# A new order of work on ScalarE, VectorE and GpSimd ahead of the tile loop, and the last expert call in two halves

## The chip, the cores and the metric

The kernel runs on one core of one Trainium2 chip. The metric is the device time of one execution in microseconds (us). Three runs of the kernel before gave a median of 718.08 us.

## The reference

The input is x with 8 x 256 rows of 512 numbers. Three sublayers follow each other; each adds to x what it computes from the layer norm of x. The first and the third are a mixture of 64 rank-16 experts, the second is a gated feed-forward layer in which the smaller half of each row's gate values is set to zero.

```
def ffn(x, A, B, Wr):                     # 64 experts of rank 16, the best 16 of each row
    scores = x @ Wr.T
    top_vals, top_idx = top_k(scores, 16)
    G = scatter(softmax(top_vals), top_idx)
    h = einsum('nd,krd->nkr', x, A)
    return einsum('nkr,kdr->nd', h * G[:, :, None], B) * 2.0

def attn(x, w_gate, w_up, w_down):        # I = 1376
    s = silu(x @ w_gate.T)
    s = where(|s| is among the 688 smallest of its row, 0, s)
    s = s * (x @ w_up.T)
    return s @ w_down.T

x = x + 0.5 * ffn(layernorm(x), A, B, Wr)
x = x + attn(layernorm(x), w_gate, w_up, w_down)
x = x + 0.5 * ffn(layernorm(x), A, B, Wr)
```

## The kernel before

**Tiles and precision.** The 2048 rows are 16 tiles of 128 rows (`NT = 16`). Every tile t passes sublayer 1, 2 and 3, in the code `j = 1, 2, 3`. Each operand of a matmul is held as two float16 numbers, an upper half (`hi`, made on ScalarE by `split_hi`, `x_to_hi`, `p_to_hi`, `v_to_hi`) and a lower half, the difference (`lo`, made on VectorE by `split_lo`, `x_to_lo`, `p_to_lo`, `v_to_lo`). A product takes three matmuls: hi by hi, lo by hi, hi by lo. Weights are scaled by their norm first: `square` and `norms` make the sums of squares, `read_norm` reads them, GpSimd's `make_scale` and `make_inverse` make the factors.

**The steps of a tile.** In sublayer 1 or 3: `norm_stats`, `rstd` (GpSimd), `norm_apply`, the two halves, `turn_x` (a transposing DMA that SyncE issues), `experts` (scores, then two blocks of 512 columns of the product with A), `choose`, `exps` and `route` for the weights of the experts, `apply_route` for the product `routed`, its halves, `turn_p` and `combine` (the product with B), then `add_ffn`. In sublayer 2: `gates` (1376 columns, three blocks), `tanh`, `silu` (VectorE; the result is what the code calls `gate_ready`), `ups` (three blocks), `gated` (the product `val`; `gated_begun` and `gated_ended` do its first two blocks and the third apart), `magnitude`, the search, `select`, `mask`, `check`, `v_to_hi`, `v_to_lo`, `turn_v`, `down` and `add_down`.

**The search** finds for every row the threshold below which values are zeroed. GpSimd's `aim` sets a first guess. Then seven counts on ScalarE (`count(t, n)`, a sign with a sum) alternate with six steps on GpSimd (`search(t, n)`, four operations on 128 x 1 numbers, lines 517 to 521). Each step adds 1 to `thr_ready[t % 2]`, to which `aim` adds 1 too, so that `thr_ready[0]` is 2 after `search(0, 0)`. VectorE's `select` then takes the threshold from the last count, `mask` zeroes, and TensorE sums a flag (`sum_flags`) that `check` reads.

**Who sets the order.** It is written out by hand. Each engine's block lists its steps one after the other, and each engine does its list in that order; semaphores couple the lists. A step whose operands are late holds up all that stands behind it on its engine. SyncE's list issues the DMAs in the same way. Ahead of the loop (`for d in range(1, FULL)`, ten passes of `tile(d)`) the weights are loaded and split while the first five tiles pass sublayer 1 and tiles 0 to 2 sublayer 2; the last five tiles, a, b, c, e and f, have an order of their own. The down weights (`MD`) have six pieces; the last has 96 rows. `calls` numbers the 32 calls of sublayers 1 and 3 in order, the last one is `(3, f)`.

**PSUM.** Eight banks of 512 numbers: `DOWN` 0, `COMB` 1, `WIDE` 2 to 4, `EXP` 5 and 6, `SCORE` 7.

## Time and profile before

| | us |
|---|---|
| median of 3 runs (717.94 to 718.62) | 718.08 |
| the profiled execution | 717.54 |
| its span on the core | 715.8 |
| TensorE busy, matmuls | 691.9 (97%) |
| VectorE busy | 471.3 (66%) |
| ScalarE busy | 359.8 (50%) |
| GpSimd busy | 220.2 (31%) |

A timeline row is one operation, or several alike (xcount), with its start and its length in us from the start of the span. In brackets stands how long its engine had been idle before it and what ended that. TensorE's matmuls overlap, so their lengths add up to more than the time they take. The name after the engine is the line of the kernel; `mem` is a large buffer that holds the staged weights at first and `gate`, `val`, `masked`, their halves and some x later.

### The profile page before, as it was taken

To read this page: it belongs to the slowest core of one execution; us is meant where nothing else is said; L and a number is where in the kernel's file an instruction comes from. 1 tells how busy PE (TensorE), PEld (TensorE's weight loads), DVE (VectorE), ACT (ScalarE), POOL (GpSimd) and SP (SyncE) were. 2 spreads that over 40 slices of the span, in tenths; PEclk is the share of its full clock that TensorE was granted. 3 is DMA by queue.
4 is the path that set the end of the run, shared out by engine and by line. 5 is a ranking of instruction groups with operands and counts; after the bars stand their busy time and mean duration, and the time that the engine had idled before them with its cause. 6 is when DMAs were issued, how large, how long until landed. Compare 5 with 4: busy or idle time off the path is not lost.

```text
span 715.8 us, 10349 instructions
## 1 busy us (share of the span) xinstructions
PE 691.9 (97%) x3674; PEld 331.2 (46%) x3675; DVE 471.3 (66%) x982; ACT 359.8 (50%) x466; POOL 220.2 (31%) x545
## 2 busy tenths in 40 slices
PE   4999898999999999999999999999999999999997
PEld 3444344435444454444445444444544444444443
DVE  6999756768476666756666576566747575538862
ACT  5887775644535254452535535254462536576220
POOL 3122443532414233240423315142341423344000
PEclk9999999999999999999999999999999999999999
DMA  9969304253525163351514325242442324123442
GB/s 333 307 154 214 52 11 71 44 100 81 95 49 95 30 110 64 71 102 33 102 42 100 74 57 89 47 97 44 91 69 49 67 44 86 30 55 71 86 85 78
DMA packets 171723, 62.28 MB, mean 87 GB/s; under 512 B 163632, under 2 KB 163632, under 8 KB 171664
## 3 DMA queue, kind: packets, MB, share of 16 engines
q1 hardware_dynamic: 171664, 61.56, 40.4%
q8 instruction: 29, 0.48, 0.3%
q14 instruction: 30, 0.25, 0.1%
HBM read 16.97 MB, written 4.19 MB: 30 GB/s over the span
## 4 chain that ended last, share of the span: by engine, by line
PE 64%; ACT 9%; DVE 9%; POOL 7%; issue 5%; DMA 4%; SPq 1%; DVEq 0%; POOLq 0%; ACTq 0%
PE ps L601 12%; PE ps L602 12%; PE ps L603 12%; PE ps L716 9%; PE ps L720 9%; PE ps L717 9%; ACT signs L924 5%; POOL small L521 3%; POOL small L518 1%; DMA mem<-w_d 1%; POOL small L517 1%; DMA mem<-w_a 1%; DVE routed L1216 1%; POOL small L519 1%; ACT mem L936 1%
## 5 line engine op out<-in xcount | busy, mean ns | idle before, releaser
L924 ACT ACTIVATE signs<-mem,small 128x1376 bf16<-128x1376 f32 x112 | 161.4, 1441 | 156.1 <-POOL small L521 140.5
L716 PE MATMUL ps<-w_b_hi,pt_hi 128*128 128x512 f16 x256 | 97.0, 379 | 0.6 <-DMA pt_hi<-p_hi 0.6
L717 PE MATMUL ps<-w_b_lo,pt_hi 128*128 128x512 f16 x256 | 97.0, 379 | 0.0
L601 PE MATMUL ps<-w_a_hi,xt_f 128*128 128x512 f16 x248 | 94.0, 379 | 0.0
L602 PE MATMUL ps<-w_a_hi,xt_f 128*128 128x512 f16 x248 | 94.0, 379 | 0.0
L603 PE MATMUL ps<-w_a_lo,xt_f 128*128 128x512 f16 x248 | 94.0, 379 | 0.0
L601 PE MATMUL ps<-w_u_hi,xt 128*128 128x512 f16 (+1 forms) x192 | 69.1, 360 | 4.4 <-DVE mem L1246 4.4
L517 POOL TENSOR_SCALAR small<-small 128x1 f32<-128x1 f32 x96 | 30.8, 321 | 129.6 <-ACT signs L924 128.6
L716 PE MATMUL ps<-w_d_hi,mem 128*128 128x512 f16 x176 | 66.7, 379 | 3.0 <-DMA mem<-mem 1.8
L601 PE MATMUL ps<-w_g_hi,xt 128*128 128x512 f16 (+1 forms) x192 | 68.5, 357 | 0.9 <-DVE mem L1253 0.9
L602 PE MATMUL ps<-w_u_hi,xt 128*128 128x512 f16 (+1 forms) x192 | 69.3, 361 | 0.0
L603 PE MATMUL ps<-w_u_lo,xt 128*128 128x512 f16 (+1 forms) x192 | 69.2, 360 | 0.0
L477 POOL TENSOR_SCALAR rvar<-mv 128x1 f32<-128x1 f32 x48 | 11.7, 244 | 185.8 <-DVE mv L1161 184.3
L602 PE MATMUL ps<-w_g_hi,xt 128*128 128x512 f16 (+1 forms) x192 | 68.5, 357 | 0.0
L603 PE MATMUL ps<-w_g_lo,xt 128*128 128x512 f16 (+1 forms) x192 | 68.5, 357 | 0.0
L717 PE MATMUL ps<-w_d_lo,mem 128*128 128x512 f16 x176 | 66.7, 379 | 0.0
L720 PE MATMUL ps<-w_b_hi,pt_lo 128*128 128x512 f16 x256 | 60.5, 379 | 0.0
L907 ACT ACTIVATE mem<-mem 128x512 f16<-128x512 f32 x16 | 10.0, 627 | 99.9 <-DVE mem L1168 99.9
L521 POOL TENSOR_SCALAR small<-small,steps 128x1 f32<-128x1 f32 x96 | 54.9, 572 | 10.8 <-POOL small L519 0.2
L1282 DVE SCALAR_TENSOR_TENSOR mem<-mem,small 128x1376 f32<-128x1376 f32 x16 | 26.4, 1650 | 48.3 <-ACT signs L924 48.2
L1176 DVE TENSOR_TENSOR halves<-normed,halves 128x512 f16<-128x512 f32 x30 | 20.7, 690 | 55.8 <-ACT halves L907 55.6
L1226 DVE TENSOR_TENSOR p_lo<-routed,p_hi 128x1024 f16<-128x1024 f32 x32 | 39.0, 1219 | 17.9 <-ACT p_hi L918 17.8
(142 smaller groups left out, 1210.3 us busy)
## 6 DMA issues: line engine op xcount, KB each, us to landing
x<-x SPq DMA_DIRECT2D x14, 256.0 KB, 3.5
out<-x SPq DMA_DIRECT2D x14, 256.0 KB, 2.3
mem<-w_g SPq DMA_DIRECT2D x4, 688.0 KB, 12.5
mem<-w_u SPq DMA_DIRECT2D x4, 688.0 KB, 5.6
mem<-w_d SPq DMA_DIRECT2D x5, 512.0 KB, 6.2
mem<-w_a SPq DMA_DIRECT2D x4, 512.0 KB, 6.2
mem<-w_b SPq DMA_DIRECT2D x4, 512.0 KB, 9.3
pt_hi<-p_hi SPq DMA_TRANSPOSE x32, 3.2
```

The lines of the kernel that those rows point to most:

```text
L517: link(pool.tensor_scalar(off[h], bal[h], -7.0, None, ALU.add))
L521: pool.tensor_scalar(thr[h], move[h], steps[h][:, n:n + 1], thr[h], ALU.mult, ALU.add).then_inc(thr_ready[h], 1)
L601: pe.matmul(dst, x_hi, w_hi, start=start, stop=False)
L602: pe.matmul(dst, x_lo, w_hi, start=False, stop=False)
L603: return pe.matmul(dst, x_hi, w_lo, start=False, stop=stop)
L716: pe.matmul(dst, x_hi[:, c, :], hi[m.name][:, c, :], start=c == 0, stop=False)
L717: pe.matmul(dst, x_hi[:, c, :], lo[m.name][:, c, :], start=False, stop=False)
L720: mm = pe.matmul(dst, x_lo[:, c, :], hi[m.name][:, c, :], start=False, stop=c == chunks - 1)
L924: act.activation(signs[:, :], mags[h], ACT.Sign, bias=thr[h], scale=-1.0, accum_out=bal[h]).then_inc(counted[h], 1)
L1176: dve.tensor_tensor(halves[j][:, D:2 * D], normed[j], halves[j][:, 0:D], ALU.subtract).then_inc(x_lo_ready[j], 1)
L1226: dve.tensor_tensor(p_lo[:, :], routed[:, :], p_hi[:, :], ALU.subtract).then_inc(p_lo_ready, 1)
L1282: link(dve.scalar_tensor_tensor(out=masked[:, 0:I], in0=mag, scalar=thr[h], in1=mag, op0=ALU.is_le, op1=ALU.mult))
```

## The change

1. **ScalarE.** `tanh(0)` and `p_to_hi(4)` stand behind three of the six squares of the down weights, not all six. The first search starts ahead of `x_to_hi(2, 2)`, the upper halves of the down weights (`split_hi(MD, n)`) are spread over both first searches, and `count`, `x_to_hi`, `v_to_hi` and `exps` are in another order up to tile 2. In the end phase `tanh(e)` stands ahead of `count(c, 6)`.
2. **VectorE.** Six waits on `thr_ready` are added: ahead of `p_to_lo(4)`, of four groups of steps that begin with a lower half of the down weights, and of `mask(0)`. `p_to_lo(4)`, `x_to_lo(2, 2)` and `gated(0)` are behind the first of them. `choose` and `route` of call 5 go ahead of `silu(1)` and behind `select(0)`. `select(1)` goes ahead of `norm_apply(3, 0)`, and `mask(1)` ahead of `x_to_lo(3, 0)`.
3. **GpSimd and SyncE.** `make_inverse("gud")` stands behind three search steps, `rstd(1, LEAD)` behind two, `rstd(2, 3)` behind the second search. `turn_x(2, 3)` is issued behind `turn_v(1)`.
4. **TensorE.** `norms(MD)`, six matmuls of one column, stands behind the first block of `ups(0)`.
5. **The last call** in two halves: `apply_route`, `p_to_hi`, `combine`, `add_ffn` and `store` of call `(3, f)` each in two pieces of half the width. `combine_last` has 48 matmuls of 256 columns for 24 of 512. The two transposing DMAs stay whole.

```diff
 scored, expert_done, combined = sem("scored"), sem("expert_done"), sem("combined")
+expert_begun, routed_begun = sem("expert_begun"), sem("routed_begun")
+comb_begun, added_begun = sem("comb_begun"), sem("added_begun")
+stored_begun = sem("stored_begun")
...
         sp.dma_start(out[t * P:(t + 1) * P, :], slot(t)).then_inc(stored[t % SLOTS], 16)
+    def store_last():
+        t, w = NT - 1, D // 2
+        sp.wait_ge(added_begun, 1)
+        sp.dma_start(out[t * P:(t + 1) * P, 0:w], slot(t)[:, 0:w]).then_inc(stored_begun, 16)
+        sp.wait_ge(added, len(calls))
+        sp.dma_start(out[t * P:(t + 1) * P, w:D], slot(t)[:, w:D]
+                     ).then_inc(stored[t % SLOTS], 16)
     def turn_x(j, t):
...
     turn_p(number[1, LEAD])
-    turn_x(2, 3)
...
     turn_v(1)
+    turn_x(2, 3)
...
     store(e)
-    store(f)
+    store_last()
+    sp.wait_ge(stored_begun, 16)
...
     make_scale(MD)
+    search(0, 0)
+    search(0, 1)
+    rstd(1, LEAD)
+    search(0, 2)
     make_inverse("gud", 2.0 ** -25)
-    search(0, 0)
-    rstd(1, LEAD)
-    searches(0, 1, 2, 3, 4, 5)
+    searches(0, 3, 4, 5)
     aim(1)
-    searches(1, 0, 1, 2, 3, 4)
+    searches(1, 0, 1, 2, 3, 4, 5)
     rstd(2, 3)
-    search(1, 5)
...
                                x_hi[c], x_lo[c], c == 0, c == DC - 1)
+                if o == 0 and k == len(calls) - 1:
+                    mm.then_inc(expert_begun, 1)
...
             pe.wait_ge(val_ready, NT)
-        elif k == len(calls) - 1:
-            pe.wait_ge(added, k - 1)
...
                    16 * (k + 1), fresh).then_inc(combined, 1)
+    def combine_last():
+        k = len(calls) - 1
+        pe.wait_ge(pt_hi_loaded, 16 * (k + 1))
+        pe.wait_ge(added, k - 1)
+        pe.wait_ge(x2_ready, NT)
+        x_hi, x_lo, w = pt_hi[k % 2], pt_lo[k % 2], D // 2
+        halves_of = [(bank(b, w), slice(h * w, (h + 1) * w)) for h, b in ((0, COMB), (1, DOWN))]
+        for dst, cols in halves_of:
+            for c in range(RC):
+                pe.matmul(dst, x_hi[:, c, :], hi["b"][:, c, cols], start=c == 0, stop=False)
+                pe.matmul(dst, x_hi[:, c, :], lo["b"][:, c, cols], start=False, stop=False)
+        pe.wait_ge(pt_lo_loaded, 16 * (k + 1))
+        for (dst, cols), done in zip(halves_of, (comb_begun, combined)):
+            for c in range(RC):
+                mm = pe.matmul(dst, x_lo[:, c, :], hi["b"][:, c, cols], start=False,
+                               stop=c == RC - 1)
+            mm.then_inc(done, 1)
     def wide(m, t, fresh=False, flags_of=None, norms_of=None, begun=None, behind=None):
...
         return mm
-    def gates(t, fresh=False, norms_of=None):
+    def gates(t, fresh=False):
...
             pe.wait_ge(val_ready, t)
-        wide(MG, t, fresh, norms_of=norms_of, behind=t if early else None
+        wide(MG, t, fresh, behind=t if early else None
              ).then_inc(gate_done, 1)
-    def ups(t, fresh=False, flags_of=None):
+    def ups(t, fresh=False, flags_of=None, norms_of=None):
         pe.wait_ge(gate_ready, t + 1)
-        wide(MU, t, fresh, flags_of, begun=up_begun if t in (1, NT - 2) else None
+        wide(MU, t, fresh, flags_of, norms_of, up_begun if t in (1, NT - 2) else None
...
     combine(1, 3)
-    norms(MD)
-    ups(0, fresh=True)
+    ups(0, fresh=True, norms_of=MD)
...
     combine(3, e)
-    combine(3, f)
+    combine_last()
...
         act.activation(p_hi[:, :], routed[:, :], ACT.Copy).then_inc(p_hi_ready, 1)
+    def p_to_hi_last():
+        k = len(calls) - 1
+        act.wait_ge(routed_begun, 1)
+        act.wait_ge(pt_hi_loaded, 16 * k)
+        act.activation(p_hi[:, 0:BANK], routed[:, 0:BANK], ACT.Copy)
+        act.wait_ge(routed_ready, k + 1)
+        act.activation(p_hi[:, BANK:KR], routed[:, BANK:KR], ACT.Copy
+                       ).then_inc(p_hi_ready, 1)
     def count(t, n):
...
     exps(4)
-    for n in range(len(MD.pieces)):
+    for n in range(3):
...
     p_to_hi(4)
+    square(MD, 3)
+    square(MD, 4)
     magnitude(0)
-    x_to_hi(2, 2)
+    square(MD, 5)
...
     count(0, 0)
+    x_to_hi(2, 2)
+    count(0, 1)
     split_hi(MD, 0)
-    count(0, 1)
+    count(0, 2)
...
     x_to_hi(1, LEAD)
-    count(0, 2)
+    count(0, 3)
     split_hi(MD, 2)
-    count(0, 3)
-    split_hi(MD, 3)
     count(0, 4)
-    split_hi(MD, 4)
...
     tanh(1)
-    split_hi(MD, 5)
+    split_hi(MD, 3)
+    exps(number[1, LEAD])
...
     magnitude(1)
-    counts(1, 0, 1, 2)
+    split_hi(MD, 4)
+    count(1, 0)
+    split_hi(MD, 5)
+    counts(1, 1, 2)
     v_to_hi(0)
-    exps(number[1, LEAD])
...
     p_to_hi(number[1, LEAD])
+    count(1, 4)
     tanh(2)
-    count(1, 4)
+    count(1, 5)
     magnitude(2)
-    count(1, 5)
+    count(1, 6)
+    act.wait_ge(counted[1], ROUNDS)
+    count(2, 0)
+    x_to_hi(3, 0)
+    count(2, 1)
     x_to_hi(2, 3)
-    count(1, 6)
-    x_to_hi(3, 0)
-    act.wait_ge(counted[1], ROUNDS)
-    counts(2, 0, 1, 2)
     v_to_hi(1)
+    count(2, 2)
+    exps(number[3, 0])
     count(2, 3)
-    exps(number[3, 0])
...
     p_to_hi(number[3, a])
-    counts(c, 5, 6)
+    count(c, 5)
     tanh(e)
+    count(c, 6)
...
     exps(number[3, f])
-    p_to_hi(number[3, f])
+    p_to_hi_last()
...
             ALU.mult).then_inc(routed_ready, 1)
+    def apply_route_last():
+        k = len(calls) - 1
+        halves_of = [slice(h * BANK, (h + 1) * BANK) for h in range(2)]
+        heads = [slice(h * KE // 2, (h + 1) * KE // 2) for h in range(2)]
+        for h, (of, at, done) in enumerate(((expert_begun, 1, routed_begun),
+                                            (expert_done, k + 1, routed_ready))):
+            dve.wait_ge(of, at)
+            dve.tensor_tensor(
+                routed[:, halves_of[h]].rearrange("p (k r) -> p k r", r=RANK),
+                bank(banks_of(k) + h).rearrange("p (k r) -> p k r", r=RANK),
+                weight[:, heads[h]].unsqueeze(2).to_broadcast([P, KE // 2, RANK]),
+                ALU.mult).then_inc(done, 1)
     def p_to_lo(k):
...
                                  ).then_inc(added, 1)
+    def add_last():
+        k, w = len(calls) - 1, D // 2
+        for h, (of, at, b, done) in enumerate(((comb_begun, 1, COMB, added_begun),
+                                               (combined, k + 1, DOWN, added))):
+            x = slot(NT - 1)[:, h * w:(h + 1) * w]
+            dve.wait_ge(of, at)
+            dve.scalar_tensor_tensor(out=x, in0=bank(b, w), scalar=unscale_f, in1=x,
+                                     op0=ALU.mult, op1=ALU.add).then_inc(done, 1)
     def add_down(t):
...
     read_norm(MD)
+    add_ffn(1, 3)
+    norm_stats(1, LEAD)
+    dve.wait_ge(thr_ready[0], 2)
     p_to_lo(4)
-    add_ffn(1, 3)
     x_to_lo(2, 2)
-    norm_stats(1, LEAD)
+    gated(0)
+    norm_apply(1, LEAD)
+    dve.wait_ge(thr_ready[0], 4)
     split_lo(MD, 0)
-    norm_apply(1, LEAD)
-    gated(0)
     x_to_lo(1, LEAD)
+    dve.wait_ge(thr_ready[0], 5)
...
     make_unscale(unscale_m, "gud")
+    add_ffn(1, 4)
+    dve.wait_ge(thr_ready[0], 6)
     split_lo(MD, 2)
-    add_ffn(1, 4)
-    split_lo(MD, 3)
-    split_lo(MD, 4)
+    read_scores(LEAD)
+    choose(number[1, LEAD])
...
     select(0)
+    route(number[1, LEAD])
+    dve.wait_ge(thr_ready[1], 2)
     mask(0)
-    read_scores(LEAD)
...
     gated_ended(1)
-    choose(number[1, LEAD])
+    dve.wait_ge(thr_ready[1], 3)
+    split_lo(MD, 3)
+    split_lo(MD, 4)
+    apply_route(number[1, LEAD])
...
     split_lo(MD, 5)
-    route(number[1, LEAD])
-    apply_route(number[1, LEAD])
+    p_to_lo(number[1, LEAD])
     silu(2)
-    p_to_lo(number[1, LEAD])
     norm_stats(2, 3)
-    norm_apply(2, 3)
...
     norm_stats(3, 0)
-    x_to_lo(2, 3)
+    select(1)
     norm_apply(3, 0)
+    mask(1)
     x_to_lo(3, 0)
-    select(1)
-    mask(1)
+    norm_apply(2, 3)
...
     add_ffn(1, LEAD)
+    choose(number[3, 0])
     v_to_lo(1)
-    choose(number[3, 0])
+    x_to_lo(2, 3)
...
     route(number[3, f])
-    apply_route(number[3, f])
+    apply_route_last()
...
     add_ffn(3, e)
-    add_ffn(3, f)
+    add_last()
 def kernel(**inputs):
```

ScalarE from the upper half of the last up weights to the second count of tile 0. L882 (before) is `square`, L931 `tanh`, L918 `p_to_hi`, L936 `magnitude`, L907 `x_to_hi`, L924 `count`, L892 `split_hi`. Before:

```order
L882 ACTIVATE signs,square_sums<-mem 128x1024
L882 ACTIVATE keep,square_sums<-mem 128x1024
L882 ACTIVATE signs,square_sums<-mem 128x1024
L882 ACTIVATE keep,square_sums<-mem 128x1024
L882 ACTIVATE signs,square_sums<-mem 128x1024
L882 ACTIVATE keep,square_sums<-mem 96x512
L931 ACTIVATE mem<-ps,small 128x1376
L918 ACTIVATE p_hi<-routed 128x1024
L936 ACTIVATE mem,small<-mem 128x1376
L907 ACTIVATE halves<-normed 128x512
L924 ACTIVATE signs,small<-mem,small 128x1376
L892 ACTIVATE w_d_hi<-mem,small 128x1024
L924 ACTIVATE signs,small<-mem,small 128x1376
```

Now (L915 `square`, L974 `tanh`, L951 `p_to_hi`, L979 `magnitude`, L967 `count`, L940 `x_to_hi`, L925 `split_hi`):

```order
L915 ACTIVATE signs,square_sums<-mem 128x1024
L974 ACTIVATE mem<-ps,small 128x1376
L951 ACTIVATE p_hi<-routed 128x1024
L915 ACTIVATE keep,square_sums<-mem 128x1024
L915 ACTIVATE signs,square_sums<-mem 128x1024
L979 ACTIVATE mem,small<-mem 128x1376
L915 ACTIVATE keep,square_sums<-mem 96x512
L967 ACTIVATE signs,small<-mem,small 128x1376
L940 ACTIVATE halves<-normed 128x512
L967 ACTIVATE signs,small<-mem,small 128x1376
L925 ACTIVATE w_d_hi<-mem,small 128x1024
```

`tanh` has moved up past three squares and `magnitude` past one, and the first count stands ahead of `x_to_hi`.

VectorE from the reading of the down weights' norm to the third lower half of them. L1117 is `read_norm`, L1226 `p_to_lo`, L1233 `add_ffn`, L1176 `x_to_lo`, L1160 and L1161 `norm_stats`, L1143 `split_lo`, L1168 `norm_apply`, L1266 `gated`. Before:

```order
L1117 COPY small<-ps 128x1
L1226 TENSOR_TENSOR p_lo<-routed,p_hi 128x1024
L1233 SCALAR_TENSOR_TENSOR x<-ps,small,x 128x512
L1176 TENSOR_TENSOR halves<-normed,halves 128x512
L1160 BN_STATS stats_1<-x 128x6
L1161 BN_AGGR mv_1<-stats_1 128x2
L1143 SCALAR_TENSOR_TENSOR w_d_lo<-mem,small,w_d_hi 128x1024
L1168 TENSOR_SCALAR normed<-x,mv_1,rvar_1 128x512
L1266 SCALAR_TENSOR_TENSOR mem<-mem,ps 128x1376
L1176 TENSOR_TENSOR halves<-normed,halves 128x512
L1143 SCALAR_TENSOR_TENSOR w_d_lo<-mem,small,w_d_hi 128x1024
```

Now (L1167 `read_norm`, L1297 `add_ffn`, L1210 and L1211 `norm_stats`, L1290 `p_to_lo`, L1226 `x_to_lo`, L1340 `gated`, L1218 `norm_apply`, L1193 `split_lo`), with a wait ahead of `p_to_lo` and of each `split_lo`:

```order
L1167 COPY small<-ps 128x1
L1297 SCALAR_TENSOR_TENSOR x<-ps,small,x 128x512
L1210 BN_STATS stats_1<-x 128x6
L1211 BN_AGGR mv_1<-stats_1 128x2
L1290 TENSOR_TENSOR p_lo<-routed,p_hi 128x1024
L1226 TENSOR_TENSOR halves<-normed,halves 128x512
L1340 SCALAR_TENSOR_TENSOR mem<-mem,ps 128x1376
L1218 TENSOR_SCALAR normed<-x,mv_1,rvar_1 128x512
L1193 SCALAR_TENSOR_TENSOR w_d_lo<-mem,small,w_d_hi 128x1024
L1226 TENSOR_TENSOR halves<-normed,halves 128x512
L1193 SCALAR_TENSOR_TENSOR w_d_lo<-mem,small,w_d_hi 128x1024
```

`p_to_lo` stands behind `add_ffn` and `norm_stats`, and the first `split_lo` behind `gated` and `norm_apply`.

VectorE around the search's result for tile 1. L1160 and L1161 are `norm_stats(3, 0)`, L1282 to L1295 `select(1)`, L1168 `norm_apply(3, 0)`, L1176 `x_to_lo`, L1300 `mask(1)`. Before:

```order
L1160 BN_STATS stats_0<-x 128x6
L1161 BN_AGGR mv_0<-stats_0 128x2
L1176 TENSOR_TENSOR halves<-normed,halves 128x512
L1168 TENSOR_SCALAR mem<-x,mv_0,rvar_0 128x512
L1176 TENSOR_TENSOR mem<-mem 128x512
L1282 SCALAR_TENSOR_TENSOR mem<-mem,small 128x1376
L1284 MAX tops<-mem 128x8
```

Now (L1356 to L1369 `select(1)`, the first L1218 `norm_apply(3, 0)`, L1374 `mask(1)`, L1226 `x_to_lo(3, 0)`, the second L1218 `norm_apply(2, 3)`):

```order
L1356 SCALAR_TENSOR_TENSOR mem<-mem,small 128x1376
L1358 MAX tops<-mem 128x8
L1359 SCALAR_TENSOR_TENSOR small<-tops,small 128x1
L1361 SCALAR_TENSOR_TENSOR tops,small<-tops,small 128x8
L1363 TENSOR_SCALAR spare,small<-tops,small 128x8
L1365 SCALAR_TENSOR_TENSOR small<-small 128x1
L1369 SCALAR_TENSOR_TENSOR flag<-small 128x1
L1218 TENSOR_SCALAR mem<-x,mv_0,rvar_0 128x512
L1374 SCALAR_TENSOR_TENSOR mem<-mem,small 128x1376
L1226 TENSOR_TENSOR mem<-mem 128x512
L1218 TENSOR_SCALAR normed<-x,mv_0,rvar_0 128x512
```

`norm_apply(3, 0)` and `x_to_lo(3, 0)` have gone from ahead of `select(1)` to behind it, the latter behind `mask(1)` too.

## Rows read from the trace of the kernel before

**Rows 1.** TensorE's waits: releaser, us in total, times, longest.
```profile
PE ps L601 <- DVE mem L1246: 4.4, 3, 2.4
```

**Rows 2.** Busy us of the engines in two windows, then granted clock and DMA.
```profile
core 0: us, PE busy (x) PEld busy (x) DVE busy (x) ACT busy (x) POOL busy (x), PEclk, DMA share, GB/s
...
76.00:80.00 4.00, 4.00 (x12) 1.51 (x11) 3.74 (x8) 3.23 (x5) 1.94 (x3) 0.58 0.34 66
...
200.00:550.00 350.00, 350.00 (x1871) 168.20 (x1869) 226.08 (x480) 156.78 (x202) 105.69 (x258) 1.00 0.37 71
```

**Rows 3.** TensorE's timeline, first passes, and one block in the loop.
```profile
71.32 1.89 PE L720 MATMUL ps<-w_b_hi,pt_lo 128*128 128x512 f16 x8
...
75.75 0.49 PE L601 MATMUL ps<-w_u_hi,xt 128*128 128x512 f16 x1 [2.42 <-DVE mem L1246]
...
84.42 0.38 PE L716 MATMUL ps<-w_b_hi,pt_hi 128*128 128x512 f16 x1
...
103.98 0.38 PE L601 MATMUL ps<-w_u_hi,xt 128*128 128x512 f16 x1 [1.72 <-DVE mem L1246]
...
111.84 0.38 PE L601 MATMUL ps<-w_g_hi,xt 128*128 128x512 f16 x1 [0.70 <-DVE mem L1253]
...
120.15 0.38 PE L716 MATMUL ps<-w_d_hi,mem 128*128 128x512 f16 x1 [1.18 <-issue]
...
146.92 0.38 PE L716 MATMUL ps<-w_d_hi,mem 128*128 128x512 f16 x1 [1.79 <-DMA mem<-mem]
...
554.32 0.38 PE L601 MATMUL ps<-w_u_hi,xt 128*128 128x512 f16 x1
...
561.28 0.19 PE L601 MATMUL ps<-w_r_hi,xt_f 128*128 128x64 f16 x1
```

**Rows 4.** ScalarE's timeline, first passes.
```profile
72.69 1.39 ACT L931 ACTIVATE mem<-ps,small 128x1376 f32<-128x1376 f32 x1
...
113.55 1.44 ACT L924 ACTIVATE signs<-mem,small 128x1376 bf16<-128x1376 f32 x1 [1.46 <-POOL small L521]
```

**Rows 5.** VectorE's timeline: `select(1)`, `mask(1)`, a `silu` in the loop, the last addition.
```profile
132.97 1.64 DVE L1282 SCALAR_TENSOR_TENSOR mem<-mem,small 128x1376 f32<-128x1376 f32 x1
...
137.34 1.64 DVE L1300 SCALAR_TENSOR_TENSOR mem<-mem,small 128x1376 f32<-128x1376 f32 x1
...
550.40 1.59 DVE L1246 SCALAR_TENSOR_TENSOR mem<-mem,ps 128x1376 f32<-128x1376 f32 x1
...
712.34 0.75 DVE L1233 SCALAR_TENSOR_TENSOR x<-ps,small,x 128x512 f32<-128x512 f32 x1 [5.19 <-PE ps L720]
```

**Rows 6.** VectorE's timeline: two operations beside the search.
```profile
93.89 1.28 DVE L1143 SCALAR_TENSOR_TENSOR w_d_lo<-mem,small,w_d_hi 128x1024 f16<-128x1024 f32 x1 [2.19 <-ACT w_d_hi L892]
...
631.81 0.68 DVE L1176 TENSOR_TENSOR mem<-mem 128x512 f16<-128x512 f32 x1
```

**Rows 7.** GpSimd's timeline: the last operation of three search steps.
```profile
93.89 1.41 POOL L521 TENSOR_SCALAR small<-small,steps 128x1 f32<-128x1 f32 x1
...
113.18 0.33 POOL L521 TENSOR_SCALAR small<-small,steps 128x1 f32<-128x1 f32 x1
...
630.21 2.34 POOL L521 TENSOR_SCALAR small<-small,steps 128x1 f32<-128x1 f32 x1
```

**Rows 8.** TensorE's timeline past 600 us.
```profile
618.29 0.39 PE L601 MATMUL ps<-w_u_hi,xt 128*128 128x512 f16 x1 [0.24 <-DVE mem L1246]
...
625.04 0.18 PE L790 MATMUL ps<-flag,ones 128*128 128x1 bf16 x1 [1.39 <-DVE x L1239]
...
627.20 0.38 PE L601 MATMUL ps<-w_g_hi,xt 128*128 128x512 f16 x1 [0.17 <-DVE mem L1253]
...
650.20 0.18 PE L790 MATMUL ps<-flag,ones 128*128 128x1 bf16 x1 [0.63 <-DVE x L1239]
...
706.95 0.39 PE L716 MATMUL ps<-w_b_hi,pt_hi 128*128 128x512 f16 x1 [0.59 <-DMA pt_hi<-p_hi]
```

**Rows 9.** DMA issues from 40 to 165 us: median us from issue to landing.
```profile
mem<-mem SPq DMA_TRANSPOSE x4, 3.7
...
xt_f<-mem SPq DMA_TRANSPOSE x1, 2.9
```

## The prediction

> **What bounds the kernel now.** I read four views, in this order. The windows come first: from 200 to 550 us TensorE is busy for all 350.00 us [rows 2], so in the loop over tiles nothing but TensorE sets the time, and a new order on other engines can win only outside it. The waits by engine say who holds TensorE up outside: the doubled gate values (`silu`, on VectorE) are its largest releaser past the weights' load, 4.4 us in three waits [rows 1]. TensorE's timeline then places the waits, and the timelines of the other engines tell what stood ahead of each releaser. Matmuls of 512 columns start 0.2155 us apart while each is listed with 0.38 us (eight take 1.89 us [rows 3]), so a listed idle time of x costs x + 0.16 us of progress. On that scale the losses up to the second `down` are:
>
> `ups(0)`: the last eight matmuls before it begin at 71.32, so the next is due at 73.04, and the block is over at 84.42: 11.38 us. A block of as many matmuls in the loop takes 561.28 - 554.32 = 6.96 us [rows 3]. The rest is 4.4 us: some 2.7 us of waiting, and 1.7 us because the granted clock was 0.58 from 76 to 80 us, most of it the 1.2 GHz level, after TensorE had stood idle [rows 2, 3]. Some 0.15 us of it is the squares' sums, which stay: 4.25 us. `ups(1)`: 1.72 + 0.16 = 1.88. `gates(2)`: 0.86. `down(0)`: 1.34. `down(1)`: 1.95 [rows 3]. Together 10.3 us.
>
> **The change, first passes.** I walk the new orders by hand from 68 us on, with the durations of the trace of before. `tanh(0)` ran at 72.69 [rows 4], behind six squares of the down weights that waited for their loads. Now it stands behind three and starts when `gates(0)` is over, about 68.1. VectorE reaches `silu(0)` after the third lower half of the up weights, about 70.9, and takes 1.59 us [rows 5], so it is ready at 72.5, ahead of the 73.04 at which TensorE wants it. The fourth lower half is ready at 74.1 and wanted at 75.0; the squares are done at 74.7, and their sums, now behind the first block of `ups(0)`, are wanted at 75.6. Loss now 0, and without the idle time I expect no drop of the clock: minus 4.25 us. `ups(0)` then ends near 80.2.
>
> The search of tile 0 is a loop of a count on ScalarE and four small steps on GpSimd. Undisturbed a round is 1.46 us of idle time ahead of the count and 1.5 us for the count with its read-out, 3.0 us [rows 4]. At 93.89 GpSimd's last step, which takes 0.33 us at 113.18, took 1.41 us, and a lower half of the down weights began on VectorE at the same 93.89 for 1.28 us [rows 6, 7]. At 630.21 it took 2.34 us, until just after a VectorE operation that ended at 632.49 [rows 6, 7]. So GpSimd stands still while such an operation runs, and through two in a row. The new waits start these halves right behind a step, when ScalarE counts and GpSimd has nothing to do: 1.1 us less in each of three rounds. The second count moves to 78.5 (GpSimd first makes the down scale) and the sixth ends near 93. `gates(1)` ends at 92.7, so `tanh(1)` runs to about 94.4 and `silu(1)` to 96.0; `ups(1)` is due at 97.9. Loss 0: minus 1.88 us. VectorE's first wait holds up `p_to_lo(4)`, `x_to_lo(2, 2)` and `gated(0)` queued behind it. `p_to_lo(4)` is out at 79.7, its transposed copy lands near 83.0 and `combine(1, 4)` wants it at 83.65: 0.6 us of cover. `gated(0)` is not wanted before 85.4.
>
> `gates(2)` waits for `gated_begun(1)`, behind `select(0)` and `mask(0)`; the mask now waits for the first step of the next search, near 102.7. The values are ready near 105.6 and due at 104.9: it keeps some 0.85 us (bounds 0.4 and 1.4). `down(0)` needs the transposed upper values: 108.7 plus 3.7 us [rows 9] is 112.4, due 112.7. Loss 0 (bounds 0 and 1). The two lower halves put off to there run back to back, 2.4 us, straight into a step of the search for tile 1. As at 630.21, the step loses those 2.4 us, and `select(1)` starts near 122.9. (The Trainium skill, SBUF — State Buffer, section SBUF: two separate sides, says that a VectorE operation with two SBUF inputs holds, for its whole length, a port pair that GpSimd's reads need. Both rows agree. If the pair were merely shared and the step lost nothing, the next paragraph's wait would be 0 and the sum 1.0 us larger.)
>
> `experts(3, 0)` is new on the list. VectorE now does `select(1)` (132.97 to 137.34 before) ahead of `norm_apply(3, 0)`, and `mask(1)`, 1.64 us, ahead of `x_to_lo(3, 0)` [rows 5], so x goes to its transposition at about 130.1 and lands 2.9 us later [rows 9], at 133.0. TensorE, now early, wants it at 132.0: it waits 1.0 us (bounds 0 and 2.5). In return `down(1)`, whose values land near 137.1, waits no more (due 138.6): minus 1.95. On SyncE's queue `turn_x(2, 3)` now stands behind `turn_v(1)`; its x is wanted only near 151.
>
> Sum of the first passes: 10.3 - 0.85 - 1.0 = 8.4 us (bounds 10.3 - 0.4 = 9.9 and 10.3 - 1.4 - 1.0 - 2.5 = 5.4). The moved `make_inverse`, `exps`, `choose` and `rstd` cost nothing: GpSimd and VectorE do them while ScalarE counts, and without that cover each would cost under 1 us of one round.
>
> **The end.** `tanh(e)` goes ahead of `count(c, 6)`. `ups(e)` waited 0.24 us for `silu(e)`, its flag sum 1.39 us for `add_down(b)` behind `select(c)` and `mask(c)`, `gates(f)` 0.17 us, and the flag sum of `experts(3, b)` 0.63 us [rows 8]. `silu(e)` comes 1.5 us earlier and `select(c)` some 2.8 us, since it had stood behind `silu(e)`. All four go: 0.40 + 1.55 + 0.33 + 0.79 = 3.1 us (bounds 1.5 and 3.1). Next in line is `down(f)`, its values landing about 0.9 us ahead of it.
>
> **The last call.** Its first half is routed and rounded while TensorE does the second, so behind the last expert matmul half an operation of each remains, and the transposition starts 1.1 us earlier. The wait of 0.59 us [rows 8], 0.75 of progress, goes, for the combine before it then bounds. The last addition falls from 0.75 [rows 5] to about 0.42 us: 0.33. The 48 matmuls of 256 columns replace 24 of 512, and no row has that width: scaled from 512 they cost the same 5.2 us; at the 0.149 us that one of 352 columns takes by the 6.96 us block [rows 3] they would cost 2.0 us more. I take 0, since 352 columns already scale with their width from 512. The final store is half as large; I count nothing. Sum 1.1 us (bounds -0.9 and 1.4). The Trainium skill, DMA: Bandwidth & Descriptors, section Anatomy of one DMA, gives for GpSimd's kind of queue a fixed 2.0 us plus bytes over 436 GB/s; by it the half store would give 0.3 us more, an estimate that no row here bears out.
>
> **Sum.** 8.4 + 3.1 + 1.1 = 12.6 us. The profiled execution took 717.54 us (span 715.8), so it becomes 704.9; the median of the runs, 718.08, is 0.54 us above it: 705.5 us. With about half of each term's spread this case spans 703.3 to 708.0.
>
> **The rivals.** *New waits for old* (0.2): the walk is too kind where it has under 1 us of cover, at the copy of `p_to_lo(4)`, at `down(0)` and at `experts(3, 0)`. Those covers speak for it; against it, that GpSimd's stalls do leave the rounds. It gives the low bound of the first passes with most of the end: 718.08 - 5.4 - 2.4 - 1.0 = 709.3. *The end does not follow* (0.1): `down(f)` or the searches of e and f bind as soon as TensorE is earlier, and half of 3.1 us comes: 707.1. *It doesn't do what it says* (0.03): VectorE is the late one at each wait, the order of ScalarE changes nothing, and only the last call gains: 717.0. *Slower* (0.04): the searches enter the loop later against TensorE and the lag does not die out. In the loop `silu` ends at 551.99 and its `ups` starts at 554.32 [rows 3, 5], so past a lag of 2.3 us every one of ten passes pays. At 1.5 us each that is 15 - 12.6 = 2.4 us slower, 720.5. By my walk the searches enter 1 us behind at most, and VectorE and ScalarE are busy 226 and 157 of 350 us [rows 2].
>
> **How the numbers follow.** The forecast has 0.63, at 705.5. The range, 702.8 to 710.0, holds it and most of the first two rivals. About 0.2%, 1.4 us, is what a measurement here can tell from no change. Faster by more: 0.63 + 0.2 + 0.1 = 0.93; same 0.03; slower 0.04.
>
> **What would show it.** In the changed kernel `ups(0)` should start at 73.0 with a granted clock of 1.00 behind it; no wait ahead of `ups(1)` and `down(0)`; some 0.9 us at `gates(2)` and 1 us at `experts(3, 0)`; `down(1)` at 138.6 and not 146.9; no flag sum waiting past 600 us; TensorE busy throughout the loop; the last combine without a gap. The forecast is wrong if `silu(0)` comes after 73.0, if two or more new waits of over 1 us stand between 80 and 150 us, or if any wait recurs in every pass of the loop.

## The result, and the profile after

The changed kernel takes **705.31 us** (median of four runs, 704.84 to 706.07), the kernel before 718.01 beside it (717.82 to 718.62): ratio 0.9823, 95% interval 0.9806 to 0.9840. Measured again later it took 705.34 us (five runs, 704.46 to 705.65) against 717.78. The forecast was 705.5, range 702.8 to 710.0.

The profiled execution of the changed kernel took 706.07 us with a span of 704.3; for the kernel before these are 717.54 and 715.8.

TensorE's timeline after, at the places that stood in [rows 3] and [rows 8] (columns: start in us, duration, engine, line, operation, output from inputs, shape, count, and in brackets the idle time before it and its releaser):

```profile
74.23 0.38 PE L616 MATMUL ps<-w_u_hi,xt 128*128 128x512 f16 x1
...
76.82 0.29 PE L630 MATMUL ps<-square_sums,ones 128*128 128x1 bf16 x6
...
81.35 0.38 PE L733 MATMUL ps<-w_b_hi,pt_hi 128*128 128x512 f16 x1
...
84.97 1.25 PE L737 MATMUL ps<-w_b_hi,pt_lo 128*128 128x512 f16 x5
...
99.20 0.38 PE L616 MATMUL ps<-w_u_hi,xt 128*128 128x512 f16 x1
...
106.60 0.38 PE L616 MATMUL ps<-w_g_hi,xt 128*128 128x512 f16 x1 [0.24 <-DVE mem L1327]
...
113.57 0.38 PE L733 MATMUL ps<-w_d_hi,mem 128*128 128x512 f16 x1
...
133.67 0.20 PE L616 MATMUL ps<-w_r_hi,xt_f 128*128 128x64 f16 x1 [0.64 <-DMA xt_f<-mem]
...
139.21 0.38 PE L733 MATMUL ps<-w_d_hi,mem 128*128 128x512 f16 x1
...
640.02 0.18 PE L824 MATMUL ps<-flag,ones 128*128 128x1 bf16 x1 [0.47 <-DVE x L1313]
...
696.02 0.27 PE L765 MATMUL ps<-w_b_hi,pt_hi 128*128 128x256 f16 x1
```

These are the starts of `ups(0)`, its sums of squares, `combine(1,4)` and the lower half of that, then `ups(1)`, `gates(2)`, `down(0)`, `experts(3,0)`, `down(1)`, the flag sum in `experts(3,b)` and the last `combine`. Rows without a bracket waited for nothing that the list shows. The waits of 2.42, 1.72, 0.70, 1.18 and 1.79 us of [rows 3] have become 0, 0, 0.24, 0 and 0; 0.64 us at `experts(3,0)` is new; of the four at the end and the one at the last combine [rows 8], one of 0.47 is left.

The windows of the same kernel (busy time of each engine with its instructions, the granted clock, the share and rate of the DMAs), for [rows 2]:

```profile
core 0: us, PE busy (x) PEld busy (x) DVE busy (x) ACT busy (x) POOL busy (x), PEclk, DMA share, GB/s
73.00:76.00 3.00, 3.00 (x16) 1.35 (x15) 2.89 (x5) 2.89 (x7) 0.78 (x2) 1.00 0.46 87
76.00:80.00 4.00, 4.00 (x26) 1.96 (x25) 2.01 (x7) 1.95 (x4) 1.96 (x7) 1.00 0.00 0
...
200.00:550.00 350.00, 350.00 (x1869) 168.06 (x1868) 226.02 (x484) 162.31 (x209) 107.09 (x258) 1.00 0.39 73
```

The granted clock from 76 to 80 us is 1.00 where it was 0.58, and the loop is still TensorE's alone.

One thing in these absolute times is no part of the change: the first 27 us, whose code is the same, came out about 1.2 us later. The first matmul on the transposed x starts at 27.51 us, in the profiled execution of before at 26.33; the twelve runs below have 26.56 to 27.59, edits of the kernel before among them (27.35 and 27.39). So 1.19 us is taken off below wherever a start after is set against a start before.

### The profile page after: what moved, and what is told of

Same layout as the page of the kernel before. It is cut to its first block, busy times and chain, and to the rows that moved or that the text cites. A ratio compares the mean times of both kernels' runs of the same rounds, so it can differ in the third digit from the quotient of the medians.

```text
span 704.3 us, 10405 instructions
## 1 busy us (share of the span) xinstructions
PE 689.8 (98%) x3699; PEld 333.9 (47%) x3699; DVE 471.7 (67%) x984; ACT 359.6 (51%) x467; POOL 217.9 (31%) x545
## 4 chain that ended last, share of the span: by engine, by line
PE 74%; POOL 7%; ACT 6%; issue 5%; DVE 5%; DMA 2%; SPq 0%; DVEq 0%; POOLq 0%; ACTq 0%
PE ps L616 14%; PE ps L617 14%; PE ps L618 14%; PE ps L733 10%; PE ps L737 10%; PE ps L734 10%; ACT signs L967 5%; POOL small L535 2%; POOL small L532 2%; POOL small L531 1%; DMA mem<-w_a 1%; POOL small L533 1%; DMA xt_f<-halves 1%; DVE mem L1356 1%; DVE tops L1358 1%
## 5 line engine op out<-in xcount | busy, mean ns | idle before, releaser
L967 ACT ACTIVATE signs<-mem,small 128x1376 bf16<-128x1376 f32 x112 | 161.4, 1441 | 152.9 <-POOL small L535 135.6
L734 PE MATMUL ps<-w_b_lo,pt_hi 128*128 128x512 f16 x248 | 94.0, 379 | 0.0
L733 PE MATMUL ps<-w_b_hi,pt_hi 128*128 128x512 f16 x248 | 94.0, 379 | 0.0
L940 ACT ACTIVATE mem<-mem 128x512 f16<-128x512 f32 x16 | 10.0, 627 | 101.0 <-DVE mem L1218 101.0
L1356 DVE SCALAR_TENSOR_TENSOR mem<-mem,small 128x1376 f32<-128x1376 f32 x16 | 26.4, 1651 | 49.5 <-ACT signs L967 49.3
L1226 DVE TENSOR_TENSOR halves<-normed,halves 128x512 f16<-128x512 f32 x30 | 20.7, 691 | 56.6 <-ACT halves L940 56.6
L737 PE MATMUL ps<-w_b_hi,pt_lo 128*128 128x512 f16 x248 | 58.6, 379 | 0.0
L535 POOL TENSOR_SCALAR small<-small,steps 128x1 f32<-128x1 f32 x96 | 52.3, 544 | 10.8 <-POOL small L533 0.2
L1290 DVE TENSOR_TENSOR p_lo<-routed,p_hi 128x1024 f16<-128x1024 f32 x32 | 39.0, 1219 | 19.0 <-ACT p_hi L951 17.2
```

What stands on the lines that cost most here:

```text
L535: pool.tensor_scalar(thr[h], move[h], steps[h][:, n:n + 1], thr[h], ALU.mult, ALU.add).then_inc(thr_ready[h], 1)
L733: pe.matmul(dst, x_hi[:, c, :], hi[m.name][:, c, :], start=c == 0, stop=False)
L734: pe.matmul(dst, x_hi[:, c, :], lo[m.name][:, c, :], start=False, stop=False)
L737: mm = pe.matmul(dst, x_lo[:, c, :], hi[m.name][:, c, :], start=False, stop=c == chunks - 1)
L967: act.activation(signs[:, :], mags[h], ACT.Sign, bias=thr[h], scale=-1.0, accum_out=bal[h]).then_inc(counted[h], 1)
L1226: dve.tensor_tensor(halves[j][:, D:2 * D], normed[j], halves[j][:, 0:D], ALU.subtract).then_inc(x_lo_ready[j], 1)
```

## The experiments

Twelve kernels ran: eleven short edits of the kernel before or of the changed one, and the changed kernel once more. Ratios are against the kernel before, run beside each on the same chip. Where a text says how far a kernel lies above the changed one, it subtracts 705.31 us from its median. The kernel before had medians of 717.67 to 718.33 us beside them, so some tenths of such a difference are not the edit's. By the ratios, each with an interval of about 1 us to either side, the old tanh order costs 3.9 us and not 3.3, the exchange at tile 1 2.7 and not 3.1, the whole store 0.4 and not 0.9; the others differ by 0.2 us or less.

### The tanh moved, alone

In the kernel before:

```diff
-            for n in range(len(MD.pieces)):
+            for n in range(3):
                 square(MD, n)
             tanh(0)
             p_to_hi(4)
+            square(MD, 3)
+            square(MD, 4)
             magnitude(0)
+            square(MD, 5)
...
-            norms(MD)
-            ups(0, fresh=True)
+            ups(0, fresh=True, norms_of=MD)
```

> The kernel before, with one part of the change: tanh(0) and p_to_hi(4) behind three squares of the down weights, and the sums of squares behind the first block of ups(0). My theory: ups(0) starts on time, 4.25 us are won there, but the search of tile 0 gets only about 3 us earlier and keeps its stalls on GpSimd, so the wait at ups(1) grows from 1.72 to about 2.8 us; total about 3.1 us less than before, 714.9. Rival (the parts add up, each by itself): 4.25 us less, 713.8, with ups(1) waiting 1.72 as before.

Measured: 716.05 us (714.93 to 716.30, six runs) against 717.96, ratio 0.9971 (0.9959 to 0.9983). A gain of 1.9 us, less than either expectation. `ups(0)` did what was expected: it starts at 74.07 without a wait and `combine(1,4)` at 81.19, 4.2 us earlier once the late start is taken off. The next two fences show where it went. TensorE's timeline of this kernel:

```profile
102.58 0.58 PE L601 MATMUL ps<-w_u_hi,xt 128*128 128x512 f16 x1 [3.55 <-DVE mem L1248]
102.96 0.63 PE L602 MATMUL ps<-w_u_hi,xt 128*128 128x512 f16 x1
103.38 0.63 PE L603 MATMUL ps<-w_u_lo,xt 128*128 128x512 f16 x1
```

and its windows:

```profile
76.00:80.00 4.00, 4.00 (x27) 2.00 (x26) 3.17 (x6) 2.38 (x4) 2.34 (x4) 1.00 0.08 17
...
104.00:112.00 8.00, 8.00 (x32) 3.37 (x30) 5.95 (x12) 3.25 (x6) 4.07 (x10) 0.71 0.00 0
```

`ups(1)` now waits 3.55 us for `silu(1)` where it waited 1.72 [rows 3], and the matmuls behind it start 0.43 us apart, at the 1.2 GHz level, until 108.5: fourteen intervals, 2.9 us more than at 0.2155. The low clock left `ups(0)` and came back at `ups(1)`. The waits at `gates(2)` and `down(0)` are gone in this kernel and the one at `down(1)` is 1.18 us, which gives back part of it: of 4.2 us, 2.3 were left at `down(1)`, and at the end 1.9. The step that failed is the one that I took over from the prediction without its companion: a wait is only won if the chain that feeds the **next** wait comes earlier too.

### The idle time before ups(0) filled

Forty-two small matmuls into a bank that nobody reads, which take up the wait of the kernel before, so that only the clock differs:

```diff
             norms(MD)
+            pe.wait_ge(scores_read, 5)
+            for _ in range(42):
+                pe.matmul(bank(SCORE, P), ones[:, :], ones[:, :], start=True, stop=True)
             ups(0, fresh=True)
```

> The kernel before, with 42 matmuls of 128 columns of ones (into the score bank, their result is not used) between norms(MD) and ups(0), where TensorE idles for 2.4 us; they take about 2.4 us. My theory: the engine does not fall to 1.2 GHz, ups(0) runs its nine first matmuls at 0.2155 us and not 0.43, and the block ends 1.7 us earlier; some of it is lost again at ups(1), whose silu is not earlier, so the wait there grows from 1.72 towards 3.4 us: total 0 to 0.5 us less than before, though the block itself gains 1.7 us. Rival (the low clock has another cause than the idle time): ups(0) runs as slowly as before, 8.67 us from its first matmul to the next block.

Measured: 718.21 us (717.82 to 718.86, ten runs) against 718.33 (fifteen), ratio 0.9997 (0.9988 to 1.0006): no change clear of noise, as the theory had it (0 to 0.5 us). Two windows of its trace:

```profile
76.00:80.00 4.00, 4.00 (x30) 2.18 (x28) 3.74 (x8) 2.81 (x4) 0.90 (x3) 1.00 0.34 66
...
104.00:112.00 8.00, 7.12 (x21) 2.70 (x22) 6.76 (x12) 4.57 (x7) 3.13 (x6) 0.60 0.00 0
```

The filling did keep the clock at 1.00 through `ups(0)`, whose block took 6.98 us and not the rival's 8.67, and it bought 1.9 us there (`combine(1,4)` at 83.61 after a start 1.06 us late, before 84.42). `ups(1)` then waited 3.42 us in place of 1.72 and ran at the low clock itself; at `down(1)` the gain was 0.1 us. So the 1.7 us that I put down to the clock in [rows 2] cost the kernel before next to nothing by itself. It was won in the changed kernel because everything behind it moved as well.

### The waits on thr_ready taken out

```diff
-            dve.wait_ge(thr_ready[0], 2)
...
-            dve.wait_ge(thr_ready[0], 4)
...
-            dve.wait_ge(thr_ready[0], 5)
...
-            dve.wait_ge(thr_ready[0], 6)
...
-            dve.wait_ge(thr_ready[1], 2)
...
-            dve.wait_ge(thr_ready[1], 3)
```

> The changed kernel without its six waits on thr_ready on VectorE; the order of all engines is kept. My theory: the lower halves of the down weights and p_to_lo(4) run as soon as their operands are there, in the same time as GpSimd's steps; three or four steps take 1.1 us more each, tanh(1) comes about 3 us later and uses up 1.8 us of slack at ups(1), so ups(1) waits again for about 1.5 us and gates(2) for more; total 1.5 to 3 us more than the changed kernel, 707 to 708.5. Rival (the new order alone does it, the waits are only a guard): within 0.5 us of the changed kernel, 705.3.

Measured: 709.46 us (709.22 to 709.52, four runs), ratio 0.9881 (0.9866 to 0.9896), 4.1 us above the changed kernel, where at most 3 were expected. The longest of GpSimd's steps in this kernel's search of tile 0 (undisturbed 0.19 to 0.34 us):

```profile
78.97 1.82 POOL L532 TENSOR_SCALAR small<-small 128x1 f32<-128x1 f32 x1
...
86.18 1.14 POOL L531 TENSOR_SCALAR small<-small 128x1 f32<-128x1 f32 x1 [0.72 <-ACT signs L967]
...
88.53 1.24 POOL L535 TENSOR_SCALAR small<-small,steps 128x1 f32<-128x1 f32 x1
...
92.44 1.40 POOL L535 TENSOR_SCALAR small<-small,steps 128x1 f32<-128x1 f32 x1
```

VectorE's operations at the same times, still of this kernel:

```profile
78.89 1.21 DVE L1290 TENSOR_TENSOR p_lo<-routed,p_hi 128x1024 f16<-128x1024 f32 x1
80.01 0.68 DVE L1226 TENSOR_TENSOR halves<-normed,halves 128x512 f16<-128x512 f32 x1
...
88.28 1.28 DVE L1193 SCALAR_TENSOR_TENSOR w_d_lo<-mem,small,w_d_hi 128x1024 f16<-128x1024 f32 x1
...
92.42 1.28 DVE L1193 SCALAR_TENSOR_TENSOR w_d_lo<-mem,small,w_d_hi 128x1024 f16<-128x1024 f32 x1 [0.92 <-ACT w_d_hi L925]
```

The first step stands still until 80.79, through the one operation (to 80.10) and the next (to 80.69); the last until 93.84 against VectorE's 93.70. And TensorE pays where the forecast says that the rounds of the search end, at `silu(1)` and behind it:

```profile
101.53 0.38 PE L616 MATMUL ps<-w_u_hi,xt 128*128 128x512 f16 x1 [2.26 <-DVE mem L1320]
...
110.69 0.38 PE L616 MATMUL ps<-w_g_hi,xt 128*128 128x512 f16 x1 [1.67 <-DVE mem L1327]
```

Those two, 0 and 0.24 us in the changed kernel, with 0.16 for each listed wait, make 3.85 of the 4.1 us: `down(1)` begins 3.8 us later than in the changed kernel. The six waits do no work and are worth a third of the gain, since they put VectorE's two-input operations where GpSimd has nothing to do.

### The old order of the tanh, in the changed kernel

```diff
-            for n in range(3):
+            for n in range(len(MD.pieces)):
                 square(MD, n)
             tanh(0)
             p_to_hi(4)
-            square(MD, 3)
-            square(MD, 4)
             magnitude(0)
-            square(MD, 5)
...
-            ups(0, fresh=True, norms_of=MD)
+            norms(MD)
+            ups(0, fresh=True)
```

> The changed kernel with tanh(0) behind all six squares and norms(MD) ahead of ups(0), as before; every other part of the change stays. My theory: the loss of 4.25 us at ups(0) comes back (2.4 us of idle time and 1.7 us of low clock), the search starts some 2 to 3 us later only, so the waits at gates(2) and experts(3, 0) shrink: 3.0 to 3.6 us more than the changed kernel, about 708.6. Rival (parts add up): 4.25 us more, 709.5.

Measured: 708.59 us (708.03 to 709.99, four runs) against 717.67, ratio 0.9878 (0.9861 to 0.9894), 3.3 us above the changed kernel. The wait is back on TensorE's timeline:

```profile
76.61 0.39 PE L616 MATMUL ps<-w_u_hi,xt 128*128 128x512 f16 x1 [2.17 <-DVE mem L1318]
```

and this is the window around it:

```profile
76.00:80.00 4.00, 3.39 (x16) 1.58 (x17) 3.74 (x8) 2.69 (x3) 1.09 (x3) 1.00 0.34 66
```

The early tanh and the rest of the first passes need each other: it is worth 1.9 us on the kernel before and 3.3 us on top of the rest. The number came out as expected, the reason only in part. The waits at `gates(2)` and `experts(3,0)` did not shrink (0.26 and 0.63 us, in the changed kernel 0.24 and 0.64), and in this profiled execution, the fastest of its four, the clock stayed at 1.00 behind the 2.17 us of idle time, so the trace has 2.3 us of the loss. Two of the other three executions (708.49 and 709.99 us) have a mean clock of 0.998. Whether a low clock at `ups(0)` is what they lose more, no trace shows.

### The tile-1 step exchanged on VectorE

The new wait at `experts(3,0)` stands behind `mask(1)`; this exchange should take it away. In the changed kernel:

```diff
             norm_apply(3, 0)
-            mask(1)
             x_to_lo(3, 0)
+            mask(1)
```

> The changed kernel with x_to_lo(3, 0) ahead of mask(1) on VectorE (norm_apply(3, 0) still behind select(1)). My theory: x goes to its transposition about 1.0 us earlier, the wait of 0.64 us at experts(3, 0) (0.81 of progress) goes, mask(1) ends 0.6 us later and down(1) is still on time: 0.8 us less than the changed kernel, 704.5. Rival: the later mask(1) makes down(1) wait, and nothing is won.

Measured: 708.41 us (708.38 to 708.55, four runs), ratio 0.9860: **3.1 us slower** than the changed kernel and not 0.8 faster. The wait at `experts(3,0)` did go, and a larger one came up 15 us later:

```profile
147.61 0.39 PE L733 MATMUL ps<-w_b_hi,pt_hi 128*128 128x512 f16 x1 [2.48 <-DMA pt_hi<-p_hi]
```

`combine(3,0)` needs the upper half of the routed product, which ScalarE converts behind a count. The changed kernel there, in the order VectorE, GpSimd, ScalarE:

```profile
136.84 1.63 DVE L1435 TENSOR_TENSOR mem<-mem 128x1408 f16<-128x1408 f32 x1
...
136.30 0.34 POOL L535 TENSOR_SCALAR small<-small,steps 128x1 f32<-128x1 f32 x1
...
132.41 1.38 ACT L986 ACTIVATE mem<-mem 128x1408 f16<-128x1408 f32 x1
...
136.67 1.44 ACT L967 ACTIVATE signs<-mem,small 128x1376 bf16<-128x1376 f32 x1 [0.17 <-POOL small L535]
...
141.49 1.04 ACT L951 ACTIVATE p_hi<-routed 128x1024 f16<-128x1024 f32 x1
```

and with the exchange:

```profile
136.29 1.63 DVE L1435 TENSOR_TENSOR mem<-mem 128x1408 f16<-128x1408 f32 x1
...
136.41 2.30 POOL L535 TENSOR_SCALAR small<-small,steps 128x1 f32<-128x1 f32 x1
...
132.52 1.38 ACT L986 ACTIVATE mem<-mem 128x1408 f16<-128x1408 f32 x1 [0.40 <-DVE spare L1429]
...
138.74 1.44 ACT L967 ACTIVATE signs<-mem,small 128x1376 bf16<-128x1376 f32 x1 [2.78 <-POOL small L535]
...
143.16 1.04 ACT L951 ACTIVATE p_hi<-routed 128x1024 f16<-128x1024 f32 x1
```

(The first line of ScalarE is `v_to_hi(1)`.) In the changed kernel GpSimd's step ends at 136.64 and the two-input copy `v_to_lo(1)` starts at 136.84. The execution with the exchange runs 0.55 us ahead of that of the changed kernel up to here (`down(0)` at 113.02 and 113.57, without a wait in either). With these 0.55 us added, its copy at 136.29 stands where it stood. What has moved is the step: `mask(1)` is behind `x_to_lo(3, 0)` now, so `v_to_hi(1)` on ScalarE is 0.66 us later, so are the count behind it and the step, which begins 0.12 us behind the copy and takes 2.30 us in place of 0.34. On the same scale the next count comes 2.6 us later, and the conversion 2.2. A margin of 0.2 us, which nobody had placed there, carries the changed kernel past this spot (0.20 us in its second profiled execution too, 136.43 to 136.63). Behind the wait of 2.48 us the clock also fell in this trace: `combine(3,0)` takes 6.87 us, without a low clock 5.18, and the granted clock from 147 to 154.5 us is 0.77.

### Two more orders of the same stretch

Both fixes, that is the exchange above and the fifth `split_hi` behind `count(1,0)`, for the 0.24 us at `gates(2)`:

```diff
             magnitude(1)
-            split_hi(MD, 4)
             count(1, 0)
+            split_hi(MD, 4)
             split_hi(MD, 5)
```

> As the one before, and on ScalarE split_hi(MD, 4) behind count(1, 0), so that the first count of tile 1 starts 0.5 us earlier and with it mask(0) and gated_begun(1). My theory: the wait at gates(2) (0.24 us, 0.40 of progress) goes too: 1.2 us less than the changed kernel, 704.1. Rival: split_hi(MD, 4) and (MD, 5) together push the second count back and down(0) waits instead; no gain beyond the kernel before this one.

Measured: 707.60 us (707.21 to 709.36, four runs), ratio 0.9856. The wait at `gates(2)` went, and `combine(3,0)` waited 2.40 us, as above.

The search of tile 1 in the order of the kernel before:

```diff
-            select(1)
             norm_apply(3, 0)
-            mask(1)
             x_to_lo(3, 0)
+            select(1)
+            mask(1)
...
-            count(2, 0)
             x_to_hi(3, 0)
+            count(2, 0)
             count(2, 1)
```

> The changed kernel with norm_apply(3, 0) and x_to_lo(3, 0) ahead of select(1) again on VectorE, and x_to_hi(3, 0) ahead of count(2, 0) on ScalarE. My theory: x for experts(3, 0) is there in time, the wait of 0.64 us goes, and down(1) is still on time or waits under 0.5 us, since the search of tile 1 is early now whatever the order of these two: 0.3 to 0.8 us less than the changed kernel. Rival (select(1) ahead is what freed down(1)): down(1) waits 1 to 2 us again, 0.5 us or more above the changed kernel.

Measured: 707.49 us (707.23 to 707.69, four runs), ratio 0.9856. Again no wait at `experts(3,0)`, and 2.63 us at `combine(3,0)`: VectorE's copy starts at 137.09, GpSimd's step at 137.29 and takes 2.21 us. `down(1)` does not wait, so the rival is right about the size of the loss and wrong about its place. The new order of `select(1)` is worth 2.2 us, by way of this collision and not by way of `experts(3,0)`, where it costs 0.8.

### The queue on ScalarE tested, and the changed kernel again

If the late conversion is the cause of the 2.4 us, it needs only to stand ahead of the count, since VectorE has its input ready at 140.4. On top of both fixes:

```diff
-            count(2, 4)
             p_to_hi(number[3, 0])
+            count(2, 4)
```

> The kernel is that of both fixes (the lower half of x for experts(3,0) ahead of mask(1) on VectorE, the fifth upper half of the down weights behind count(1,0) on ScalarE), with one more exchange on ScalarE: the upper half of the routed product for combine(3,0) ahead of count(2,4) instead of behind it. In the trace of both fixes TensorE waits 2.40 us at combine(3,0) for the transposing DMA of that half; the half is converted by ScalarE behind a count that ends about 1.7 us later than in the changed kernel, though VectorE has the product ready about 2.7 us before. If that queue is the whole cause, the conversion runs about 2.7 us earlier and its DMA, behind the one of x on SP's queue, about 2.3 us earlier: combine(3,0) waits 0 to 0.3 us, the span is 703.0 to 703.6 us in an execution whose start is like that one's, and the median 705.0 to 705.6, 0 to 0.9 below the changed kernel's in the same call, which the two earlier gains (0.26 at gates(2), 0.8 at experts(3,0)) then leave. Rival: the transfers of VectorE's lower half, or the search of pass 2 that is now one conversion later, end last; then a wait of 1 us or more stays at combine(3,0) or comes up at gates(3), and the median is 706.3 or more.

Beside it the changed kernel without an edit:

> The changed kernel as it is, on the same chip as the run above, so that the two are compared directly: 705.3 to 706.0 us. Rival: the level differs from chip to chip, and the kernels that came out 2 to 3 us above it did so for that reason and not for the wait of 2.4 to 2.6 us at combine(3,0); then this one is at 707 us or more here.

Measured side by side: 706.02 us (705.40 to 706.27, five runs) with the edit, ratio 0.9834 (0.9821 to 0.9848); 705.34 (704.46 to 705.65, five runs) for the changed kernel, ratio 0.9824 (0.9810 to 0.9837). ScalarE and TensorE of the edited kernel:

```profile
140.67 1.06 ACT L951 ACTIVATE p_hi<-routed 128x1024 f16<-128x1024 f32 x1 [0.17 <-DVE routed L1266]
...
145.67 0.39 PE L733 MATMUL ps<-w_b_hi,pt_hi 128*128 128x512 f16 x1 [0.32 <-DMA pt_hi<-p_hi]
...
188.82 0.39 PE L733 MATMUL ps<-w_b_hi,pt_hi 128*128 128x512 f16 x1 [0.18 <-DMA pt_hi<-p_hi]
```

The wait fell from 2.40 to 0.32 us, which confirms that the queue on ScalarE is where it comes from (the blocked step, 2.27 us here, is what made the queue late), and the median by 1.6. It lies between what the theory and the rival gave. The changed kernel was as fast here as in its first measurement, so a level that shifts from one measurement to the next does not explain the 2 to 3 us of the variants. But the edited kernel, 0.44 us ahead of the changed one at this point (145.67 to 146.11), was not faster at the end. By `ups(3)` it was 0.15 ahead (163.66 to 163.81), by the combine at 188.8 it was 0.20 behind, and a flag sum at 639.97 waited 0.44 us that in this execution of the changed kernel waited for nothing. The search of tile 2 still starts late, behind the blocked step. By this reading, which no run tests, it is once more the first lesson: TensorE alone was moved forward. None of the variants beats the changed kernel.

### The end in the old order

```diff
-            count(c, 5)
+            counts(c, 5, 6)
             tanh(e)
-            count(c, 6)
```

> The changed kernel with tanh(e) behind count(c, 6) again, as before. My theory: the waits past 600 us come back (0.24, 1.39 and 0.17 us, and 0.6 in place of 0.47), total 2.4 us more than the changed kernel, 707.7. Rival (those waits were due to where the search stood against TensorE, and with TensorE 8 us earlier they are different): under 1 us more, or over 3.5.

Measured: 707.73 us (706.74 to 708.80, four runs), ratio 0.9859 (0.9844 to 0.9874), 2.4 us above the changed kernel. TensorE's waits from 605 us on, in this kernel:

```profile
610.34 0.39 PE L616 MATMUL ps<-w_u_hi,xt 128*128 128x512 f16 x1 [0.26 <-DVE mem L1319]
...
617.08 0.18 PE L824 MATMUL ps<-flag,ones 128*128 128x1 bf16 x1 [1.39 <-DVE x L1312]
...
619.24 0.38 PE L616 MATMUL ps<-w_g_hi,xt 128*128 128x512 f16 x1 [0.17 <-DVE mem L1326]
```

Those are three of the four of [rows 8], to 0.02 us, and 2.3 us of progress with 0.16 for each. The one exchange on ScalarE accounts for them. The fourth, the flag sum near 640 us (0.63 us before), did not come back in this trace, so its part of the gain does not hang on the exchange.

### The last call whole, and the last store whole

The last call whole again: `combine_last`, `p_to_hi_last`, `apply_route_last`, `add_last` and `store_last` replaced by the whole steps.

```diff
-            combine_last()
+            combine(3, f)
...
-            p_to_hi_last()
+            p_to_hi(number[3, f])
...
-            apply_route_last()
+            apply_route(number[3, f])
...
-            add_last()
+            add_ffn(3, f)
...
-            store_last()
-            sp.wait_ge(stored_begun, 16)
+            store(f)
```

> The changed kernel with its last call whole, as before: apply_route, p_to_hi, combine, add_ffn and store in one piece each. My theory: the last combine waits 0.59 us again (0.75 of progress), the last addition takes 0.75 for 0.48 us and the last store some 0.3 us longer: 1.3 to 1.4 us more than the changed kernel, 706.7. Rival (the 48 narrower matmuls cost what the earlier start gives): within 0.3 us of the changed kernel.

Measured: 706.46 us (705.67 to 706.62, five runs), ratio 0.9839 (0.9825 to 0.9852), 1.15 us above the changed kernel. TensorE waits 0.56 us before the last combine again.

Only the store whole:

```diff
                 sp.wait_ge(added_begun, 1)
-                sp.dma_start(out[t * P:(t + 1) * P, 0:w], slot(t)[:, 0:w]).then_inc(stored_begun, 16)
                 sp.wait_ge(added, len(calls))
-                sp.dma_start(out[t * P:(t + 1) * P, w:D], slot(t)[:, w:D]
-                             ).then_inc(stored[t % SLOTS], 16)
+                sp.dma_start(out[t * P:(t + 1) * P, :], slot(t)).then_inc(stored[t % SLOTS], 16)
```

> The changed kernel, but the last tile is stored by one DMA of 256 KB behind both half additions; all else stays in halves. My theory: the store of half the width shortens the time from issue to the end by about 0.35 us, so this kernel takes 0.35 us more than the changed one. Rival (a store has a fixed price whatever its size): no difference, within 0.1 us from the last addition to the end of the span.

Measured: 706.18 us (705.88 to 706.67, five runs) against 718.33, ratio 0.9828 (0.9815 to 0.9841). The issue of the last store on SyncE's queue, of the changed kernel and then of this one:

```profile
701.97 0.33 SPq L352 DMA_DIRECT2D out<-x  x1
```

```profile
701.91 0.33 SPq L351 DMA_DIRECT2D out<-x  x1
```

The spans end at 704.3 and 704.5: 2.3 and 2.6 us after the last issue, so the half store is worth about 0.3 us in the traces. The medians differ by 0.9, and the two kernels' runs lie as far apart among themselves; as ratios to the kernel before beside each (0.9828 and 0.9823) they differ by 0.4 us, near the 0.3 of the traces.

## Point by point

**What bounds the kernel.** Right. The loop from 200 to 550 us is TensorE's for 350.00 us before and after, and all of the gain lies outside it. The lag of the searches, which the slower rival lived on, does not show: no wait recurs.

**The sum.** All in progress of TensorE, the late start taken off:

| term | forecast | measured | from |
|---|---|---|---|
| `ups(0)` | 4.25 | 4.26 | 84.42 + 1.19 - 81.35 |
| `ups(1)` | 1.88 | 1.88 | no wait |
| `down(0)`, `down(1)` | 1.34 + 1.95 | 1.34 + 1.95 | no waits |
| `gates(2)` | 0.86 - 0.85 | 0.86 - 0.41 | wait of 0.24 |
| `experts(3,0)` | -1.0 | -0.81 | wait of 0.64 |
| `combine(1,4)` | 0 | -0.17 | lower half at 84.97, due 84.80 |
| first passes | 8.4 | 8.9 | 146.92 + 1.19 - 139.21 |
| the end | 3.1 | 2.5 | wait of 0.47 left |
| the last call | 1.1 | 1.3 | below |
| sum | 12.6 | 12.7 | |

Less the 1.19 us of the late start this is 11.5, the difference of the two spans. In the second profiled execution of the changed kernel the end has no wait, the span is 703.4 and the difference 12.4, or 13.4 with its late start of 1.0 us taken off. That the total came within 0.1 to 0.8 us is in part luck: the terms are off by +0.5, -0.6 and +0.2 us, and the signs cancel. One statement of the sum does not follow from its own bounds. With half of each term's spread the case spans 704.6 to 708.8 us, and even the full bounds do not reach 703.3.

**The first passes.** The walk held to 0.5 us. *`gates(2)`* was sized from `mask(0)` at 102.7 + 1.19; it started at 103.55, and the values came 0.4 us earlier than I had them. *The cover of 0.6 us* at `p_to_lo(4)` was not there: the lower half was out at 81.20, 0.3 us later than walked (79.7 + 1.19), its copy landed some 3.7 us after the issue at 81.22 where I had 3.3, and the combine lost 0.17. *The two lower halves back to back* did block the next search as foreseen, though for 1.7 us and not 2.4, in two steps of 1.19 and 1.00 us in place of 0.30 and 0.19. *Two more blocked steps* the forecast did not have: 1.80 us at 113.48, through the last lower half of the down weights and `p_to_lo` behind it, and 2.06 us at 128.12, beside `mask(1)`. They found slack: `select(1)` began at 123.58, on the forecast's scale 122.4 for 122.9. *The term of the clock* was right in the sum and wrong in what I made of it. It counted as 1.7 us by its own right; the filled kernel shows that alone it is worth 0.1.

**GpSimd's stalls.** Right, and the six waits are worth 4.1 us by themselves, more than the 3.3 that three rounds of 1.1 us would give. The Trainium skill, SBUF — State Buffer, section SBUF: two separate sides, has a VectorE operation with two SBUF inputs hold a port pair that GpSimd's reads need, as an exclusive lock. The trace agrees here too: the steps of 1.82 and 1.40 us above end 0.10 and 0.14 us after VectorE does. It also says that there is no sharing, and of the steps shown here none got through such an operation. By the Trainium skill's section whichever of the two starts first has the pair. There the rows differ: the step at 630.21 [rows 7] began, by the profile's start times, 0.06 us ahead of VectorE's copy, and was the one that stood still, while the copy took as long as elsewhere. VectorE in the kernel before:

```profile
630.27 1.63 DVE L1361 TENSOR_TENSOR mem<-mem 128x1408 f16<-128x1408 f32 x1 [0.94 <-ACT mem L943]
```

**The end.** The mechanism was right, and the old order brought back the three waits to 0.02 us. The term was mis-sized by 0.6 us, the flag sum at 640.02, which the forecast had go. In the second execution it did. The difference is a collision again. In the first execution GpSimd's step:

```profile
620.01 2.34 POOL L535 TENSOR_SCALAR small<-small,steps 128x1 f32<-128x1 f32 x1
```

in the second:

```profile
619.46 1.80 POOL L535 TENSOR_SCALAR small<-small,steps 128x1 f32<-128x1 f32 x1
```

The two-input copy begins at 619.98 in the first and at 619.58 in the second, and a second such operation follows it. The step that began 0.12 us ahead of the copy ended just behind it at 621.26; the one that began 0.03 us behind it stood through both. The next count is 1.1 us later (622.38 to 621.29), and so is `add_down(c)`, which the flag sum waits for. The forecast's 3.1 us and the measured 2.5 are two executions of one kernel.

**The last call.** The forecast took the cost of 48 matmuls of 256 columns as 0, with 2.0 us as the bound. They start 0.109 us apart, half of 0.2155 and a little:

```profile
699.29 0.27 PE L765 MATMUL ps<-w_b_hi,pt_hi 128*128 128x256 f16 x1
699.40 0.27 PE L766 MATMUL ps<-w_b_lo,pt_hi 128*128 128x256 f16 x1
699.51 1.91 PE L770 MATMUL ps<-w_b_hi,pt_lo 128*128 128x256 f16 x16
```

That is 0.06 us for all 48. The Trainium skill, TensorE: Matmul & The Clock Gate, section Wait — 56ns, not 53.3ns?, gives N / 2.4 GHz and about 2.5 ns from start to start at the full clock. An estimate from it is 109 ns for 256 columns, as measured. The last addition takes 0.48 us, not 0.42, and the half store, which I had counted at nothing, gives 0.3 to 0.4 us. With 0.75 for the wait and 0.21 for the addition less the matmuls it is 1.3. Here the 0.3 us, the forecast's estimate from the Trainium skill (DMA: Bandwidth & Descriptors, section Anatomy of one DMA), which it left out of its sum, was the better guide, though the Trainium skill states it for another kind of queue than this store's.

**The rivals.** *New waits for old* came in small: 0.41, 0.81 and 0.17 us of its sort, all but the last in the forecast. *The end does not follow*: it does. *It doesn't do what it says*: refuted by the old tanh order (3.3 us), the waits taken out (4.1) and the old end (2.4), each a part of the change undone. *Slower*: nothing of it.

**My own corrections** failed. The tanh alone, the exchange at tile 1, both fixes and the old search order were all expected faster than they came out, by 1 to 4 us. Each followed one wait of TensorE and took the other engines' times as given. The prediction fared better because it walked the orders of all four.

## What to carry to other kernels

When one of several waits in a row is removed, the gain is kept only if the chain that feeds the next wait is early as well; look for it first, and expect the next stage to pay in idle time and in a low clock otherwise. Place VectorE operations with two SBUF inputs where GpSimd is idle, by a wait on its last step if need be, and before moving anything by half a microsecond that such an operation or a GpSimd step waits for, list the pairs of the two that stand within that distance. Compare their times on a common scale first: two executions of this program start up to 1.2 us apart. On an engine that serves both a search and a transfer, put the conversion that a DMA waits for ahead of the count whenever its input is ready; the one run that tests this gained 1.6 us on the kernel of both fixes and nothing on the changed one.

## What I had not expected of the hardware

- A collision is decided by tenths of a microsecond. A GpSimd step beginning 0.12 us ahead of a VectorE copy took 1.80 us. Steps beginning 0.06 us ahead (at 630.21 in the kernel before) and 0.03 us behind took 2.34 us, through the next operation too; one that ended 0.2 us ahead of the copy took 0.34 us. In the two executions compared above it makes most of the difference of 0.9 us between their spans.
- The clock does not fall after every wait of that length. At `ups(0)` it was 0.58 of full speed behind 2.42 us of idle time in the kernel before, and 1.00 behind 2.17 us with the old tanh order; at `ups(1)` 1.00 behind 2.26 us without the six waits, 0.71 and 0.60 behind 3.55 and 3.42 us. The length alone does not decide: at `combine(3,0)` the matmuls ran at the 1.2 GHz level for a while behind 2.48 us (the exchange at tile 1) and at full speed behind 2.40 and 2.63 us (both fixes, the old order of `select(1)`). What decides is open.
- The low clock costs a kernel less than its rows say. Of 42 executions of the kernel before, the six with a mean clock of 1.000 have a median of 717.9 us and the others of 718.2: 0.3 us, where the rows give 1.7. The six alone spread over 0.8 us, so the 0.3 is not clear of noise, and 1.7 would be.
